# First attention: 44 instead of 56 of the first batch's 64 score maxima stand ahead of the second scores

## The reference

```python
def _L0_attn_ref(x, W_qkv):                       # 16 heads of 8 dimensions
    q, k, v = (heads(t) for t in jnp.split(x @ W_qkv, 3, axis=-1))
    scores = jnp.einsum('bhnd,bhmd->bhnm', q, k) / jnp.sqrt(128.0)
    attn = jax.nn.softmax(scores, axis=-1)
    return jnp.einsum('bhnm,bhmd->bhnd', attn, v)   # heads put together again

x = _layernorm(x + _L0_attn_ref(x, W_qkv))
x = _layernorm(x + _L0_ffn_ref(x, ...))   # 32 experts, top 6, and a shared one
x = _layernorm(x + _L1_attn_ref(x, ...))  # sigmoid attention
x = _layernorm(x + _L1_ffn_ref(x, ...))
```

## Time and profile before

| | us |
|---|---|
| median of 3 runs (lowest to highest) | 1024.18 (1024.17 to 1026.49) |
| the profiled execution's own time | 1023.77 |
| its span, first to last instruction | 1021.7 |
| first second scores on PE (L683) | 51.51 |
| last maximum's bank handed on (DVE) | 348.86 |
| first expert matmul on PE | 385.69 |

### The profile page before, as it was taken

The page is one execution under the profiler, slowest core; times in us unless marked ns, Lnnn a source line. Parts: engine busy times, 40 slices in busy tenths (PEclk is TensorE's granted clock), DMA queues, the critical chain, the costliest instruction groups (busy, mean ns, idle before and its releaser), DMA issues. The chain is left out here.

```text
span 1021.7 us, 20122 instructions
## 1 busy us (share of the span) xinstructions
PE 979.9 (96%) x5769; PEld 469.4 (46%) x5769; DVE 826.8 (81%) x1811; ACT 732.8 (72%) x945; POOL 523.6 (51%) x631
## 2 busy tenths in 40 slices
PE   8999999999999999999999999999999999999996
PEld 4422222222222246888888887863232333222585
DVE  7999999999999867889788789987666666644677
ACT  4377887878888776655555555668889888999753
POOL 3051744726538745677677676675443144310275
PEclk9999999999999999999999999999999999999999
DMA  7661223122130005323433432443422332230011
GB/s 229 205 226 48 81 64 109 45 87 95 40 109 17 3 4 165 122 87 127 143 99 95 154 115 80 151 147 98 150 87 68 92 123 73 66 108 1 1 32 52
DMA packets 73548, 97.04 MB, mean 95 GB/s; under 512 B 12620, under 2 KB 42188, under 8 KB 73100
## 3 DMA queue, kind: packets, MB, share of 16 engines
q1 hardware_dynamic: 73496, 96.40, 29.7%
HBM read 68.18 MB, written 27.79 MB: 94 GB/s over the span
## 5 line engine op out<-in xcount | busy, mean ns | idle before, releaser
L780 DVE TENSOR_REDUCE a_nmax<-a_ps_f 128x1 f32<-128x512 f32 x512 | 319.7, 683 | 7.7 <-PE a_ps_f L627 5.3
L542 ACT ACTIVATE a_prob<-a_ps_s 128x1024 f32<-128x1024 f32 x256 | 250.0, 1022 | 63.5 <-PE a_ps_s L683 62.3
L1428 ACT ACTIVATE a_prob<-a_ps_s 128x1024 f32<-128x1024 f32 x256 | 244.4, 1026 | 27.8 <-PE a_ps_s L1480 26.8
L2248 POOL TENSOR_TENSOR moe_hl<-moe_hid,moe_hh 128x512 fp32r<-128x512 f32 x134 | 174.2, 1305 | 84.1 <-ACT moe_hh L2129 84.0
L627 PE MATMUL a_ps_f<-a_ks,a_qs 48*128 48x512 bf16 x512 | 156.9, 384 | 10.7 <-DVE a_nmax L780 3.1
L2119 ACT ACTIVATE moe_ps<-moe_ps 128x512 f32<-128x512 f32 x128 | 74.5, 582 | 111.6 <-PE moe_ps L2042 110.8
L1493 PE MATMUL a_ps_o<-a_prob,a_va 128*32 128x512 f32 x1024 | 136.4, 605 | 1.8 <-DVE a_turned_o L1608 1.2
L696 PE MATMUL a_ps_o<-a_prob,a_va 128*32 128x512 f32 x1024 | 136.4, 605 | 0.5 <-ACT a_prob L542 0.4
L683 PE MATMUL a_ps_s<-a_qs,a_ks 51*128 51x512 bf16 x512 | 131.8, 381 | 1.7 <-ACT a_prob L542 1.4
L627 PEld LDWEIGHTS a_ps_f<-a_ks,a_qs 48*128 48x128 bf16 x512 | 38.5, 93 | 193.9 <-DVE a_nmax L780 188.1
L2170 DVE TENSOR_TENSOR moe_prod<-moe_cw,moe_ps 128x512 f32<-128x512 f32 x128 | 87.3, 682 | 27.4 <-PE moe_ps L2042 26.7
(11 more groups left out here) (324 smaller groups left out, 1636.1 us busy)
## 6 DMA issues: line engine op xcount, KB each, us to landing
moe_cw<-r_weights SPq DMA_DIRECT2D x256, 128.0 KB, 2.8
parts_q<-a_parts SPq DMA_DIRECT2D x48, 256.0 KB, 2.5
parts_k<-a_parts SPq DMA_DIRECT2D x48, 256.0 KB, 2.6
a_qs<-parts_q SPq DMA_DIRECT2D x126, 96.0 KB, 2.4
a_ks<-parts_k SPq DMA_DIRECT2D x126, 96.0 KB, 2.4
out_x<-g_X SPq DMA_DIRECT2D x7, 256.0 KB, 2.3
a_prob<-in_x_t SPq DMA_DIRECT2D x3, 512.0 KB, 5.4
moe_wg<-in_wg SPq DMA_DIRECT2D x1, 1088.0 KB, 6.7
```

The costliest lines, as they stand in the source:

```text
L542: nc.scalar.activation(prob[:, u % PSLOTS, :, :], ps_s[:, u % 2, :, :], ACT.Exp, scale=float(P) ** -0.5).then_inc(exp_done, 1)
L780: nc.vector.tensor_reduce(nmax[:, half_no, h % 2, col:col + 1], ps_f[:, bank, :], AX.X, ALU.max, negate=True).then_inc(max_done, 1)
L1428: nc.scalar.activation(prob[:, u % PSLOTS, :, :], ps_s[:, u % 2, :, :], ACT.Sigmoid, scale=float(HD) ** -0.5).then_inc(exp_done, 1)
L2248: nc.gpsimd.tensor_tensor(hl[:, part_at(j), :], hid[:, hid_at(j), :], hh[:, part_at(j), :], ALU.subtract).then_inc(hl_done, 1)
```

## The change

`LATE` goes from 8 to 20: the lead has 44 turns instead of 56 (22 units instead of 28), and the last batch's loop 20 instead of 8. Every maximum falls 12 turns later against the second scores, and what hangs on it moves along: `max1` from turn 11 to 24, `max0` from turn 47 to 58 (`o1` and `o0` stay at 9 and 46), the early products from unit 5 to 10, so that they now fill the lead's last unit, and the last batch's X turns from units 7, 9, 11, 13, 21, 23, 25 to 13, 15, ..., 25, its routing from unit 14 to 18. GpSimd splits the next batch's first maxima ahead of q and k instead of behind them (except in the lead), and SP writes `max0`'s rows ahead of the parts.

```diff
-LATE = 8
+LATE = 20
...
-EARLY_U = 5
+EARLY_U = 10
 EARLY_BANKS = 4
-MT_AT = (47, 11)
+MT_AT = (58, 24)
 OT_AT = (46, 9)
...
                 if fore and back:
                     stack(b + 1, 1 - p, NG - 1, True)
-                if qk_on:
-                    parts_to_dram(b + 2, p)
                 if fore:
                     max_rows(b + 1, 1 - p, 0)
                 if qk_on:
+                    parts_to_dram(b + 2, p)
                     sp.wait_ge(parts_out, OUT_C * (b + 3) + OUT_C)
...
-                if u1 == NU and qk_on:
+                if u1 == NU and qk_on and not back:
                     split_qk(b + 2, 0)
                     split_qk(b + 2, 1)
                 if u1 == NU and fore:
...
                     split_max(b + 1, 0)
+                    if qk_on and back:
+                        split_qk(b + 2, 0)
+                        split_qk(b + 2, 1)
...
-X_AT0 = (7, 9, 11, 13, 21, 23, 25)
+X_AT0 = (13, 15, 17, 19, 21, 23, 25)
 X_POOL = (4, 5, 6)
-EXP_AT, ROUTE_U, CT_U = 13, 14, 23
+EXP_AT, ROUTE_U, CT_U = 18, 18, 23
```

## The result

| | before | after |
|---|---|---|
| median (lowest to highest), five executions each | 1024.42 (1024.17 to 1027.66) | 1030.61 (1028.95 to 1031.82) |
| ratio of the means, 95% interval | | 1.005 (1.003 to 1.0069) |
| the profiled execution's time, span | 1023.77, 1021.7 | 1031.82, 1029.9 |

By the medians the change costs 6.2 us, by the means 5.1 (1030.47 against 1025.38), where the prediction said 5.5: slower, by more than the 0.3% that a measurement can tell. In a second set the changed kernel ran five times, at a median of 1029.26 against 1023.83 before, a ratio of 1.0053 (1.0035 to 1.007).

What follows compares the result with a forecast made beforehand. PE and DVE bound each other through three banks. Lead -6.9, last loop +8.2 and last batch's rest -5.9 give -4.6; guests +8.5 and unit 16 +1.6 make +5.5 on 1023.77: 1029.3, own range 1026.5 to 1031, overall 1021.0 to 1032.5.

Steps and rivals of the forecast that it cites:

- lead: Before the batch loops: with 22 units left, second scores start at 44.6 instead of 51.51, -6.9.
- last batch's rest: Behind the last maximum: X turns two units apart save 6.1, start 0.2 sooner, routing costs 0.4; -5.9.
- The circle of three banks: Batch loops: PE and DVE bound each other through three banks, 2.48 a pair; delays to score 3 or 4 are lost.
- the two named places: Batch loops: DVE idle some 0.7 behind turn 26 (`max1`) and 0.6 behind turn 58 (`max0`).
- guests: `max1`, `max0`, `o1`, `o0` in the bank rotation: alone 2.81 a loop against 1.6 in couples; +8.5 in all.
- the first rival: Batch loops: guests in the bank rotation cost nothing, the 8.5 is 0, time 1020.8; chance 0.14.
- Unit 16: First batch loop: PE waits 2.2 for `max1`'s rows, written behind the later weights' loads; +1.6, between 0.8 and 2.3.
- Zeros: Batch loops: `max0`'s rows (at most 3.5 in all) and the changed order on GpSimd and SP cost 0.
- -4.6: Lead, last loop and last batch's rest together, without guests and unit 16: what the move itself gains.
- 8.2: Last loop: 12 more turns ahead of the last maximum, three pairs 7.5 and the division of `o1` 0.7.

Runs made afterwards that it cites:

- the profile with the whole clock: The changed kernel again, unedited, second set: profiled execution 1028.68, clock 0.998, no fall of the clock in the first loop; median of that set 1029.26.
- the couples: Changed kernel with `o0` and `max0` at turns 54 and 55, `o1` and `max1` at 21 and 23: 1022.01, ratio to before 0.9982.
- the lone guests: Kernel before with `max1` moved to turn 12, `max0` to 50, `o0` to 42, `o1` left at 9: 1031.03, ratio 1.0077.
- With couples, and the wait on GpSimd out of the way: Changed kernel with both pairs restored, four useless matmuls, and `max0`'s split between first and second weight in the loop before the last: 1019.53, ratio 0.9953.
- the four matmuls: Changed kernel with four matmuls without use on PE right ahead of the first second scores: 1029.35, ratio 1.0052.
- the run with couples and matmuls: Changed kernel with both pairs restored (turns 54 and 55, 21 and 23) and four useless matmuls ahead of the first second scores: 1021.17, ratio 0.9965.

## Why the prediction was right, point by point

Sizes are from the profile with the whole clock, against the profiled execution of before: 1028.68 - 1023.77 = +4.9, forecast +5.5.

| step | forecast | measured | from |
|---|---|---|---|
| lead | -6.9 | -6.4 | 45.09 - 51.51 |
| first second scores to last maximum | +18.3 | +16.8 | 314.02 in place of 297.24 |
| of it, up to the next loop's `o1` | +2.7 | +1.6 | 49.37 in place of 47.77 |
| of it, five batch loops | +6.2 | +5.9 | 214.32 in place of 208.41 |
| of it, from there on | +9.4 | +9.3 | 50.33 in place of 41.06 |
| last batch's rest | -5.9 | -5.7 | 31.29 in place of 36.94 |
| sum | +5.5 | +4.7 | 390.40 - 385.69 |

- **The circle of three banks** is confirmed from four sides: loops of 42.86, the waits at the two named places, the couples that take them away (41.70), and the lone guests that bring them into the kernel before (42.77). What four lone guests cost over two couples was put a little too high, 1.23 a loop for 1.18; the excess is at `max1` and `o1`, 0.72 forecast and 0.65 had back. The Trainium skill's rule (Perfetto Trace Analysis, Optimizing Tensor Performance, Matmuls) that groups of matmuls should rotate through different banks was the first rival; with three banks the rotation did not hide the guests, as DVE's 0.62 and 0.60 show.
- **The lead**: the mechanism held, and the start was 0.49 late; 0.44 of this had come about by the last early product (43.19 on PE, 42.75 forecast). The lead's own `max0` stands among the early products, as it did before, and the sum names no term for it. With the whole clock the first scores of a unit ahead of it and behind it are on PE:

```profile
38.35 0.39 PE L626 MATMUL a_ps_f<-a_ks,a_qs 48*128 48x512 bf16 x2
...
41.49 0.39 PE L626 MATMUL a_ps_f<-a_ks,a_qs 48*128 48x512 bf16 x2
```

  These two units take 3.14, where two of 1.38 would be 2.76; so `max0` makes 0.38 of the 0.44.
- **Unit 16**: the wait is there, but 0.5 in place of 1.6; the rest of the first loop, 1.1 for its guests, came as forecast (1.6 = 1.1 + 0.5). The step that failed is the assumption that the loads would still hold SP until 64.49, with unit 16 at 65.4; both sides had moved by some 0.9.
- **The last batch's rest**: of the 9.17 from the fourth X turn to the fifth 6.16 goes (6.1 forecast), and the X turns start 0.21 sooner against the last maximum (2.97 in place of 3.18; 0.2 forecast). The routing beside them is what was put too low: the last two steps are 0.22 and 0.61 longer, 0.83 where 0.4 was taken and 2.5 allowed.
- **Zeros**: GpSimd's and SP's order (1023.92 against 1023.83) and the rows of `max0`, by which no maximum was late, were rightly put at nothing.
- **Not foreseen**: the granted clock. The one profile before had 0.999, and the prediction has no term for a fall. Executions with a clock of 0.992 to 0.995 are found in both: 4 of 10 of the changed kernel, 13 of 68 of the kernel before, whose times in those are 1025.6 to 1027.6. They make the changed kernel's first median 1.2 higher than the mean of its two other executions (1029.4), which is close to the forecast. That the 6.2 of the medians is about as near to 5.5 as the 4.9 is luck: the falls of the clock hide that the sum was too high, by the 1.1 of unit 16 above all, from which the lead's 0.5 took some back.
- **What the move is worth without the guests' price**: the forecast said -4.6. With couples, and the wait on GpSimd out of the way, 1019.53 - 1024.03 = -4.5. That kernel also has the four matmuls; by themselves they made no difference that these runs can tell (1029.35, 5.8 above the kernel before beside it; without them 1029.26, 5.4 above). By the parts of its profile it is -6.4 for the lead, +7.7 to the last maximum and -6.1 behind that, where the -4.6 is -6.9 + 8.2 - 5.9; so the two agree in part because the differences cancel. Of the 8.2 the division of `o1`, 0.7, is not in that kernel, where it stands behind the last maximum.

## What to carry to other kernels

Where a short list of buffers rotates between two engines that bound each other, the place of each guest in it has a price that no busy share shows: work out when the item gets its buffer and who stands behind it, for odd and even places apart, before moving anything past it. When a table of places is shifted, shift the guests as a group and keep their pairing, or the gain of the shift goes into the circle. And a split that waits for another engine blocks all that stands behind it in its queue: fill the wait with a piece that fits, not with nothing and not with too much.

## What the runs showed of the hardware that was not expected

TensorE's granted clock fell to 0.50 in the middle of a busy program. In the first profile PE had been idle for 0.73 us at 44.6 and then for 0.35 and 0.21, and had 1.44 of 2.00 us busy from 46 to 48; with the first of these filled it still fell, at 48 to 50. The profile with the whole clock has the same three idle stretches and the same 1.44, and a clock of 1.00 from 42 to 60. In the run with couples and matmuls the clock was whole there, and fell elsewhere, behind the 1.36 us that PE was idle for the late split:

```profile
330.00:333.00 3.00, 1.64 (x15) 0.32 (x15) 1.57 (x6) 0.69 (x2) 2.77 (x6) 1.00 0.00 0
333.00:336.00 3.00, 2.93 (x18) 0.64 (x18) 2.41 (x4) 1.94 (x2) 3.00 (x1) 0.74 0.04 8
```

There the wait of 1.40 us on DVE was followed by further waits for scores of 0.67 and 0.44. In the run with the couples alone PE was idle for the same 1.36 us at the same place, and the clock stayed at 1.00 behind it. The Trainium skill (TensorE: Matmul & The Clock Gate, A second HAM failure mode: psum-queue depth-cycling) tells of a kernel in which PE is idle for short moments between groups of matmuls, as it cycles through banks, and the clock goes between its two levels; these traces agree in so far as the longest idle stretch just ahead of either fall is 0.73 and 1.36 us. They do not settle it: the same stretches stand in profiles whose clock stayed at 1.00 behind them.
